# Output projection of attention as seven block products in a two-layer graph network

## The reference

```python
h = relu(layernorm(x))                       # layer 0
q, k, v = h @ Wq + bq, h @ Wk + bk, h @ Wv + bv
ctx = softmax(q @ k.T / sqrt(128) + (0 if adj else -9e15)) @ v    # per head
x = x + ctx @ Wf + bf                        # the output projection that is changed
h = relu(layernorm(x))                       # layer 1
hw = h @ W;  th = tanh(hw)
z = th @ w_src + (th @ w_dst).T              # per head
p = softmax(where(adj, leaky_relu(z), -999))
g = sigmoid(h @ H_w.T + H_b)
x = x + g * elu(p @ hw + b) + (1 - g) * h
```

## Time and profile before

| | us |
|---|---|
| median of 3 runs | 2498.94 |
| lowest, highest | 2498.16, 2499.29 |
| span of the profiled execution, first to last instruction | 2497.4 |
| TensorE busy | 2466.8 |
| VectorE busy | 1987.7 |
| ScalarE busy | 922.8 |
| GpSimd busy | 785.2 |

### The profile page before, as it was taken

One profiled execution on the slowest core, in us unless ns is written; L12 is line 12 of the kernel. 1 busy time (PEld: TensorE's weight loads), 2 busy tenths in 40 slices (PEclk: granted clock), 3 DMA queues, 4 the chain that ended last, 5 costly groups with the idle time before them and its releaser, 6 DMA issues.

```text
span 2497.4 us, 54938 instructions
## 1 busy us (share of the span) xinstructions
PE 2466.8 (99%) x22921; PEld 1765.1 (71%) x22952; DVE 1987.7 (80%) x2748; ACT 922.8 (37%) x1146; POOL 785.2 (31%) x558
## 2 busy tenths in 40 slices
PE   7999999999999999999999999999999999999997
PEld 6676677776777766777766777667777667776676
DVE  7878878778777788787787777887877877778868
ACT  6433333233333333333343333333333433333334
POOL 0133332333332333323333323333233333233331
PEclk9999999999999999999999999999999999999999
DMA  7344343343343443433433434434434334344332
GB/s 260 90 83 78 75 94 84 74 95 69 82 101 73 85 79 76 92 85 74 93 71 80 101 76 82 81 75 90 87 77 88 73 79 101 76 82 82 76 65 52
DMA packets 544290, 214.66 MB, mean 86 GB/s; under 512 B 509825, under 2 KB 519041, under 8 KB 544257
## 3 DMA queue, kind: packets, MB, share of 16 engines
q1 hardware_dynamic: 544256, 214.18, 39.8%
HBM read 67.03 MB, written 25.17 MB: 37 GB/s over the span
## 4 chain that ended last, share of the span: by engine, by line
PE 95%; DVE 3%; ACT 1%; issue 1%; DMA 0%; POOL 0%; SPq 0%; DVEq 0%; ACTq 0%; POOLq 0%
PE pair_prj L613 58%; PE pair_prj L637 29%; PE pair_att L653 3%; PE pair_att L734 2%; PE pair_att L750 1%; PE pair_att L793 1%; DVE w_lo L1005 1%; DMA arena<-in_L_gnn_Wq 0%; PE pair_prj L663 0%; ACT w_hi L1580 0%; PE pair_prj L779 0%; DVE w_top L967 0%; ACT w_lo L1615 0%; DVE arena L1055 0%; DVE p_place L1326 0%
## 5 line engine op out<-in xcount | busy, mean ns | idle before, releaser
L613 PE MATMUL pair_prj<-w_hi,arena 128*128 128x512 f16 (+1 forms) x6168 | 1445.5, 325 | 0.9 <-DVE w_lo L1005 0.9
L613 PE MATMUL pair_prj<-w_lo,arena 128*128 128x512 f16 (+1 forms) x3084 | 1002.8, 325 | 0.0
L613 PEld LDWEIGHTS pair_prj<-w_hi,arena 128*128 128x128 f16 x6168 | 603.4, 98 | 398.6 <-DVE w_lo L1005 1.0
L637 PE MATMUL pair_prj<-arena,w_hi 128*128 128x256 f16 x4536 | 747.8, 273 | 1.0 <-issue 1.0
L637 PE MATMUL pair_prj<-arena,w_lo 128*128 128x256 f16 x2268 | 618.2, 273 | 0.0
L637 PEld LDWEIGHTS pair_prj<-arena,w_hi 128*128 128x128 f16 x4536 | 439.6, 98 | 51.4 <-issue 1.4
L613 PEld LDWEIGHTS pair_prj<-w_lo,arena 128*128 128x128 f16 x3084 | 301.8, 98 | 192.7
L1911 POOL TENSOR_TENSOR rstd<-var_eps,minus_half 128x2 f32<-128x2 f32 x62 | 62.1, 1002 | 652.0 <-DVE var_eps L1024 645.0
L637 PEld LDWEIGHTS pair_prj<-arena,w_lo 128*128 128x128 f16 x2268 | 221.9, 98 | 25.7
L1930 POOL TENSOR_TENSOR arena<-arena,b_row 128x768 f32<-128x768 f32 x60 | 108.4, 1807 | 331.3 <-DVE arena L1092 331.3
L1584 ACT ACTIVATE h_hi<-arena,shift,rstd 128x768 f16<-128x768 f32 x124 | 120.7, 1020 | 218.4 <-DVE shift L1029 218.4
(11 more groups left out here) (216 smaller groups left out, 2866.1 us busy)
## 6 DMA issues: line engine op xcount, KB each, us to landing
arena<-in_x SPq DMA_DIRECT2D x63, 768.0 KB, 4.3
out<-arena SPq DMA_DIRECT2D x64, 384.0 KB, 2.3
arena<-arena SPq DMA_TRANSPOSE x372, 3.3
arena<-in_L_gnn_Wq SPq DMA_DIRECT2D x2, 1152.0 KB, 8.8
arena<-in_L_gnn_Wk SPq DMA_DIRECT2D x2, 1152.0 KB, 12.0
w_hi<-in_L_gnn_Wv SPq DMA_DIRECT2D x2, 1152.0 KB, 12.7
w_lo<-in_L_gnn_Wf SPq DMA_DIRECT2D x2, 1152.0 KB, 12.3
arena<-in_L_gnn_H_w SPq DMA_DIRECT2D x2, 1152.0 KB, 8.0
```

Of the source, the lines that this page charges most:

```text
L613: mm = nc.tensor.matmul(pair[:, lo:hi], lhs(a, k), weight(m, k, b)[:, lo:hi], start=(k == 0 and n == 0), stop=(k == KT - 1 and n == 2))
L637: mm = nc.tensor.matmul(pair[:, c * 256:(c + 1) * 256], weight(m, k, a)[:, o:o + P], (ht0_hi, ht0_lo)[b][:, k, :], start=(k == 0 and n == ...
```

## The change

For groups 2 to 30 (`seven(g)`) the output projection of the group, 256 x 768 by 768 x 768, is taken as a 2 x 2 block product and computed as seven products of quarter size instead of eight. The blocks are tile (rows), half of the contracted features and half of the columns. Products 0 to 6 pair these operands:

- left: C00, C01, S2, S1, C11, S0, S3, where C is the context's block (tile, half) and S0 = C10 + C11, S1 = S0 - C00, S2 = C00 - C10, S3 = C01 - S1 (`whole_sums`, with hi and lo parts by `high_sums` on ACT and `low_sums` on DVE)
- right: B11, B21, T3, T2, T4, T1, B22, where B is a block of Wf and T a sum of such blocks

Each product is 9 matmuls of 384 columns. Products 3, 4, 5 and 6 go on accumulating in the PSUM place of an earlier one. DVE adds each of the seven results to a quarter of x1 (`add_form`) in the place of two `keep_x1`.

The four T forms are made once in step 0 and 1 (`sum_term` on POOL, `high_term` on ACT, `low_term` on DVE). All eight forms, hi and lo, 288 KB each, are stored in DRAM. The place of Wf in `w_hi`, `w_lo` becomes four slots; T2 stays in slot 3, six forms are loaded in every step (`next_forms`, `late_forms` on SP), each when the product that used the slot is done. Product 6 runs in the next step, between Q half 0 and Q half 1. Q is written to `pair_att` instead of `pair_prj`, from step 2 on. The loop runs over i = 3 to 30, and step 2 is unrolled. On DVE, from step 3 on, the moments of x1 and the offset come behind `p1_low(1)`, the first Q copy-out and the last add. POOL's `add_output_bias` moves up between the products of layer 1.

```diff
+        FORMS = 8
+        B11, B21, T3, T2, T4, T1, B22, B12 = range(FORMS)
+        SLOTS = 4
+        forms = nc.dram_tensor("forms", [FORMS, 2, P, 3 * QUARTER], F16, kind="Internal").ap()
...
+        def seven(g):
+            return not isinstance(g, int) or 2 <= g <= GROUPS - 2
+        def q_pair(i, half):
+            return pair_prj[half] if isinstance(i, int) and i < 2 else pair_att[half]
...
+        def f_before(g):
+            return 2 * g if isinstance(g, int) and g < 2 else 7 * g - 10
...
-            with eng.Fori(2, GROUPS - 1) as i:
+            with eng.Fori(3, GROUPS - 1) as i:
...

+                def load_form(n, form, landed):
+                    for part in range(2):
+                        sp.dma_start(slot(n, part), forms[form, part]).then_inc(landed, DMA)
+                def next_forms():
...
+                    for n, form in enumerate((B11, B21, T3)):
+                        if not isinstance(i, int) or i != 2:
+                            after_held(sp, transposes_held, f_psum, f_before(j) + 5 + n)
+                        load_form(n, form, slot_landed[n])
+                def late_forms():
+                    for n, form in enumerate((T4, T1, B22)):
+                        after_held(sp, transposes_held, f_psum, f_before(i) + 1 + n)
+                        load_form(n, form, slot_landed[n])
...
                     sp.dma_start(rows, x_g[i + 1]).then_inc(rows_loaded, DMA)
+                if seven(i):
+                    next_forms()
...
                     transpose_rows(0, 1, ht0_lo, i + 1)
...
+                if seven(i):
+                    late_forms()
                 if mid:
                     first_probabilities(j, j + 1)

+                def form_product(g, n):
...
+                    elif n == 3:
+                        pe.wait_ge(sum_lo_made, 4 * (g - 2) + 2)
+                        pe.wait_ge(x1_ready, before + 1)
+                    elif n == 4:
+                        pe.wait_ge(ct_ready, 2 * g + 2)
+                        pe.wait_ge(x1_ready, before + 3)
+                    elif n == 5:
+                        pe.wait_ge(sum_lo_made, 4 * (g - 2) + 3)
+                        pe.wait_ge(x1_ready, before + 4)
...
+                    for k in range(3):
+                        for q, (a, b) in enumerate(((0, 0), (0, 1), (1, 0))):
+                            w = slot(n % 4, b)[:, k * QUARTER:(k + 1) * QUARTER]
+                            mm = nc.tensor.matmul(place, terms[a][:, k, :], w, start=(opens and k == 0 and q == 0),
+                                                  stop=(k == 2 and q == 2), skip_group_check=not opens)
+                    mm.then_inc(f_psum, 1)
...
-                        after(pe, x1_ready, 2 * i - 1)
-                        project_columns(WQ, 0, pair_prj[0], q_psum)
-                        after(pe, x1_ready, 2 * i)
-                        project_columns(WQ, 1, pair_prj[1], q_psum)
...
+                            pe.wait_ge(z_ready, 2 * i - 3)
+                        project_columns(WQ, 0, q_pair(i, 0), q_psum)
...
+                            if seven(j):
+                                form_product(j, 6)
+                            pe.wait_ge(z_ready, 2 * i - 2)
+                        project_columns(WQ, 1, q_pair(i, 1), q_psum)
                 if last:
+                    pe.wait_ge(q_ready, 2 * i + 1)
                     attend(0)
...
                 if last:
+                    pe.wait_ge(q_ready, 2 * i + 2)
                     attend(1)
...

+                carried = mid and (not isinstance(i, int) or i > 2)
+                if mid and not carried:
...
                     variance(1, x1, j)
...
                 if last:
                     p1_low(1, p)
                 if now:
                     dve.wait_ge(q_psum, 2 * i + 1)
+                    biased_columns(0, q_pair(i, 0), qt, bq_col, col(w_undo, WQ), q_ready)
+                if carried:
+                    add_form(j, 6)
+                    dve.wait_ge(x1_ready, f_before(j) + f_parts(j))
+                    variance(1, x1, j)
...
                 if last:
                     sum_and_invert(1, p)
+                if carried:
+                    offset(1, j)
...

+                if now and seven(i):
+                    low_sums(2, 1)
+                    low_sums(1, 2)
+                if mid:
                     gate_argument(1)
+                if now and seven(i):
+                    add_form(i, 0)
+                    last_context_low()
+                    add_form(i, 1)
+                    leak_and_mask(0, lambda: add_form(i, 2))
+                    low_sums(0, 3)
+                    shift1(0, lambda: add_form(i, 3))
+                    add_form(i, 4)
+                    leak_and_mask(1, lambda: add_form(i, 5))
+                    low_sums(3, 4)
+                    shift1(1)
+                    p1_low(0, j)
+                    sum_and_invert(0, j)
```

More of the change, by code:

```diff
@@ L939, in one @@
                     logits()
-                if now:
+                if now and seven(i):
+                    for n in range(6):
+                        form_product(i, n)
+                elif now:
                     project_output(0)
@@ L1542, in one @@
                     context_low(0)
+                if now and seven(i):
+                    for n in (0, 2, 1, 3):
+                        whole_sums(n)
                 if mid:
                     spread_over_heads(0)
-                if now:
+                if now and not seven(i):
                     context_low(1)
@@ L1555, in one @@
                     shift1(1)
-                if nxt:
+                if nxt and not seven(i):
                     keep_x1(0)
@@ L1855, in one @@
                     h_parts(1)
+                if now and seven(i):
+                    context_parts()
+                if mid:
                     gate_tanh(0)
-                if now:
+                if now and not seven(i):
                     context_high(0)
@@ L1918, in _, with sum_term @@
                 top_weight(m)
+            def sum_term(form, left, right, done, op=ALU.subtract):
+                after(pool, terms_summed, done)
+                nc.gpsimd.tensor_tensor(term_of[form], left, right, op).then_inc(terms_summed, 1)
             pool.wait_ge(eye_made, 2)
+            pool.wait_ge(weight_ready, made_ready(WF, 1))
+            sum_term(T1, term_of[T3], term_of[T1], 0)
+            sum_term(T3, term_of[T2], term_of[T3], 1)
             power(0, 1)
@@ L2002, in one, with add_output_bias @@
                     add_h(1, p)
+                def add_output_bias(t):
+                    if t == 0:
+                        pool.wait_ge(x1_loaded, DMA * (i + 1))
+                    if t == 0 and first:
+                        pool.wait_ge(bf_folded, 1)
+                    nc.gpsimd.tensor_tensor(x1[:, t, :], x1[:, t, :], bf_row[:], ALU.add).then_inc(bf_added, 1)
+                early = now and seven(i)
                 if mid:
@@ L2011, in one @@
                     if not nxt:
-                        nc.gpsimd.memset(gaps_in(end_flat), 0.0).then_inc(end_gaps, 1)
-                if now:
-                    pool.wait_ge(x1_loaded, DMA * (i + 1))
-                    if first:
-                        pool.wait_ge(bf_folded, 1)
-                    for t in range(T):
-                        nc.gpsimd.tensor_tensor(x1[:, t, :], x1[:, t, :], bf_row[:], ALU.add).then_inc(bf_added, 1)
+                        nc.gpsimd.memset(gaps_in(end_flat), 0.0).then_inc(end_cleared, 1)
+                if now and not early:
+                    add_output_bias(0)
+                    add_output_bias(1)
+                if first:
+                    sum_term(T2, term_of[T2], term_of[T1], 2)
+                    sum_term(T4, term_of[T4], term_of[T2], 3)
                 if now and not nxt:
```

275 lines of the change are left out of this document (242 added, 33 removed).

## The result

The changed kernel takes **2727.24 us** (median of 4 runs, 2724.92 to 2729.25) against 2499.11 (2498.16 to 2499.76): ratio 1.0914, 95% interval 1.0898 to 1.0929. It is slower by 228 us, 7.4 us of them in each of the 29 steps. The prediction said slower, 2678 us, with a range up to 2725; the time lies 2 us above that range. The mechanism was the forecast one, its size was not.

What follows compares the result with a forecast made beforehand. TensorE (PE), busy 99% of the span, was taken as the bound. 2497.4 + 29 x (5.0 wait + 1.0 clock) + 5 start = 2676.4, plus 1.5 from span to median, gave 2678 us; range 2590 to 2725.

Steps and rivals of the forecast that it cites:

- PE's part: TensorE's matmul work: seven products of 1.46 us replace 11.7 us of output projection, saving 1.46 us a step.
- VectorE's tail and what follows: VectorE's work behind the block products delays offset and transposes, so TensorE waits 6.0 us: +5.0 us a step.
- t: Time in us within a step, counted from where PE ends gate half 1 and starts `logits`.
- the low pair: SP's two transposes of tile 1's low probabilities, needed by `attend(1)`: issued at 31.2, landed at 35.85.
- A1: `attend(1)` of the next step on PE: reached at 35.85 instead of 30.87, after a wait of 6.0 us.
- The clock: TensorE resumes at 1.2 GHz after its wait at `attend(1)`: 1.0 us lost a step, between 0.4 and 1.7.
- The start: Making low forms on VectorE delays layer 1's low weights before the steady steps: +5 us, bounds 0 and +12.
- Sum: Whole kernel: 2497.4 + 29 x (5.0 + 1.0) + 5 = 2676.4, with 1.5 from span to median 2678 us.
- The saving: Rival, chance 0.13: no new wait at `attend(1)`, so TensorE's 42.4 us are saved: 2462 us.
- the clock did not stay up: Denies a rival, chance 0.20: the wait at `attend(1)` comes, TensorE's clock does not fall: 2649 us.
- the form loads: Rival, chance 0.08: loads in SP's queue are the bound, some 2 us a step beyond the forecast: 2736 us.
- The wait did not come out small: Denies a rival, chance 0.07: wait at `attend(1)` small, 2 us net, 2562 us.

Runs made afterwards that it cites:

- the kernel that fills PE again: Changed kernel with twelve places changed in the orders of VectorE, GpSimd and SyncE: 2491.06 us, ratio 0.9966.
- the filled kernel: Changed kernel with 46 extra matmuls of 256 columns put ahead of attention half 1, filling TensorE's wait: 2665.36 us, ratio 1.0667.
- order on VectorE: Changed kernel with the first Q copy-out, seventh block sum and moments ahead of `p1_low(1)`, the offset right behind it: 2578.37 us, ratio 1.032.
- seven edits aimed at single waits: Kernel with both orders changed, plus four moved places on VectorE (2553.13 us), then three more on GpSimd and VectorE: 2548.91 us.
- three that also took care of what ran side by side: On the kernel with those seven edits, two more moves on VectorE and one of GpSimd's additions of h: 2491.06 us, ratio 0.9966.
- order on SyncE: Changed kernel with the low transposes of tile 1 ahead of the high transpose of h half 1: 2670.4 us, ratio 1.0689.
- seventh product at the step's end: Changed kernel with the seventh product and its sum moved back from the next step to the end of their own: 2579.50 us, ratio 1.0321.
- half filled: The kernel with 46 filling matmuls ahead of attention half 1, with 23 instead: 2716.61 us, ratio 1.0875.
- both orders changed: Changed kernel with the reorderings on VectorE (moments first) and SyncE (low transposes first) together: 2556.17 us, ratio 1.0231.

## Why the prediction was off

**PE's part.** Right: seven products at 1.46 us each (9 matmuls of 0.1625), and the kernel that fills PE again has a period below the old one.

**VectorE's tail and what follows.** Right step by step, though 0.3 to 0.6 us late throughout: `p1_low(0)` at t = 14.63 for 14.3, `p1_low(1)` 20.28 for 19.9, the offset 26.54 for 26.15, the low pair issued 31.59 for 31.2, A1 36.46 for 35.85, its wait 5.9 for 6.0, 29 times. The distance to A1 grew by 5.6 for 5.0: 0.4 is a term that was left out (the gate argument starts 0.77 late, since VectorE is still at `low_sums(2, 1)` and `low_sums(1, 2)`, which stand ahead of it), and 0.24 the landing in 4.87 for 4.63. From A1 to the next t = 0 the filled kernel, at full clock, takes 45.13 us for 45.35 before; why is not shown. So 5.3 us a step are left, in sum 155 us for 145.

**The clock.** This is the step that failed, the one term outside its bounds: 1.0 us a step, 29 in all, with bounds of 0.4 and 1.7; measured 2.1 and 62. The prediction read one stint at half clock of 3.4 us from one wait, let the wait of 6 us use up part of it, and took the middle. In the changed kernel the stint was 6.8 us at 27 of the 29 waits, twice the one that was read, and PE worked through about 5.6 us of it in one step and 3.3 in the next: 2.6 and 1.5 us against the filled kernel's 45.13. The 1 to 3 us at half clock that the prediction would look for behind each wait were too few as well. Both ends of the bounds came from a single stint, behind a wait of 1.9 us, and so bounded nothing. The rule of the Trainium skill named there ("TensorE: Matmul & The Clock Gate", Part 1: the slow state is the default, activity releases it) did hold in its direction at every A1 wait of the changed kernel, and the filled wait shows it most plainly. Behind the shorter waits of the experiments the clock often stayed up.

**The start.** +5 was taken, about 10.7 came: the last offset of the next group's rows ahead of the first steady step stands at 204.75 for 194.07. PE waits 2.1 us for a low half on VectorE (until 73.93) and 2.0 us for a copy-out (until 101.87), where the kernel before has no wait, and the clock is 0.83 in the 10 us windows from 70 and from 100, for 1.00 before. GpSimd sums the four new forms for 12 us between 62 and 86. How the 10.7 us divide among these is not shown. They lie inside the bounds of 0 and 12.

**Sum**: 155 + 62 + 11 = 228 us for 145 + 29 + 5 = 179. Two thirds of the 49 us missed are the clock. Even with its upper bound, 1.7, and the two other terms as they came out the sum is 13 us short of the time: 2498.9 + 155 + 49 + 11 = 2714. The range ended at 2725, although all upper ends at once gave 2734 in the prediction's own sum; the time lies between the two.

**The rivals.** The saving did not arrive, the clock did not stay up, and the form loads did not count in the time. They were later than forecast, though: in 7 steps product 5 waited until t = 8.8 to 9.2 for T1's low half, forecast to land at 7.5, and A1's wait hid it. The wait did not come out small; the order on VectorE could have made it so.

## What to carry to other kernels

A step that is moved behind a wait on an in-order engine moves all that stands behind it: write down, for the engine that is not the bound, everything from the moved operation to the next arrival at the bound, with each round trip. Do not price a wait of TensorE by its length alone: add the work at half clock behind it, and read that from many waits of the same length or take the worst end. And ask of a second engine what it waits for: once it hardly waits for the bound any more, it may itself be the bound. Here seven edits aimed at single waits then gave 7 us together, and three that also took care of what ran side by side gave 58.

## What was not expected of the chip

- **The clock falls or not behind waits of one length**, and where it falls it is for 3.4 or for 6.8 us. Counted over whole traces (waits of TensorE, then falls of the granted clock to 0.50):

| kernel, and where TensorE waits | waits | us | falls | us at half clock |
|---|---|---|---|---|
| filled wait, A1 | 30 | 0.6 to 0.95 | 0 | |
| order on SyncE, A1 | 29 | 1.6 to 2.4 | 4 | 3.4 |
| order on VectorE, A1 | 29 | 2.0 to 2.4 | 9 | 3.4 |
| order on SyncE, low values | 24 | 2.3 | 20 | 3.4 |
| seventh product at the step's end | 29 | 2.4 to 2.8 | 2 | 3.4 |
| half filled, A1 | 29 | 2.8 to 3.5 | 24 | 3.4 (13), 6.8 (11) |
| changed kernel, A1 | 29 | 5.4 to 6.2 | 29 | 3.4 (2), 6.8 (27) |

Waits of 2.3 us cost clock in most steps of one kernel, while waits of 2.4 to 2.8 us cost it in two steps of another. Why is not shown.
- **VectorE and GpSimd hold each other up** in some operations and not in others: two subtractions of SBUF operands 1.88 us alone and 5.07 beside GpSimd, a minimum 0.56 and 2.15; statistics (0.54 to 0.56 in all 248) and copies out of PSUM (1.01) were the same beside it. It goes the other way too: with both orders changed, GpSimd's power on 2 elements takes 1.50 us where it starts just behind `p1_low(1)`, in the changed kernel's first step 0.74. In every one of these places the slow operation of VectorE reads two SBUF operands, or is the minimum that alone takes 0.56 us where others of its size take 0.96. That is the rule of the Trainium skill, "SBUF — State Buffer", section "SBUF: two separate sides": a pair of ports is shared by the two engines and locked for a whole instruction against VectorE's operations with two SBUF inputs or in a two-port mode. The rows agree with it; no run here tried the cause by itself.
